# Keys turned by VectorE and by transfers instead of by TensorE, a third score bank, and weight units dealt out anew

## The reference, cut to what matters

```python
kx, vx = split(ctx_2048 @ w_kv_x.T)          # 4096 context rows, 8 groups of 128
kx = layernorm(kx, kxln_w, kxln_b)            # over the 128 of a head
p  = softmax(q @ kx.T / sqrt(128))            # 2 heads of a group share keys and values
out = p @ vx
```

## Time and profile before

| | us |
|---|---|
| median of 3 runs | 2565.9 (2561.31 to 2568.36) |
| the profiled execution | 2565.89, its span 2564.1 |
| TensorE busy | 2278.4 (89%) |
| VectorE busy | 1792.0 (70%) |
| ScalarE busy | 1193.7 (47%) |
| GpSimd busy | 589.8 (23%) |
| wide stage, first projection to last weighing | 195.96 to about 1170 |

### The profile page before, as it was taken

The page is one execution under the profiler, slowest core; times in us unless marked ns, Lnnn a source line. Parts: engine busy times, 40 slices in busy tenths (PEclk is TensorE's granted clock), DMA queues, the critical chain, the costliest instruction groups (busy, mean ns, idle before and its releaser), DMA issues. The chain is left out here.

```text
span 2564.1 us, 31522 instructions
## 1 busy us (share of the span) xinstructions
PE 2278.4 (89%) x11472; PEld 1555.9 (61%) x11472; DVE 1792.0 (70%) x3422; ACT 1193.7 (47%) x1924; POOL 589.8 (23%) x435
## 2 busy tenths in 40 slices
PE   3778999999999999886797989788878779899998
PEld 2556666666666666564685456555546337677876
DVE  7857977887687778977775976766767764554444
ACT  4443466556565666533233114576666853211111
POOL 7810033333333333441000003313141300000000
PEclk9889999999999999998898999999999989899999
DMA  3331100010100100003445100000000023555661
GB/s 132 115 139 54 54 17 29 14 32 9 29 17 22 29 9 25 5 1 131 156 158 218 68 21 10 1 10 1 6 5 1 21 79 139 216 202 220 232 236 66
DMA packets 48438, 187.98 MB, mean 73 GB/s; under 512 B 6112, under 2 KB 10976, under 8 KB 38048
## 3 DMA queue, kind: packets, MB, share of 16 engines
q1 hardware_dynamic: 48288, 186.00, 20.1%
HBM read 175.50 MB, written 10.49 MB: 73 GB/s over the span
## 5 line engine op out<-in xcount | busy, mean ns | idle before, releaser
L407 PE MATMUL wide_a<-wide_w,ctxT 128*128 128x256 f32 (+1 forms) x2048 | 436.9, 367 | 2.8 <-POOL wide_eps L376 2.8
L407 PEld LDWEIGHTS wide_a<-wide_w,ctxT 128*128 128x128 f32 x2048 | 367.9, 191 | 77.3 <-issue 36.5
L389 POOL TENSOR_TENSOR wide_sums<-wide_sums,wide_s 128x512 f32<-128x512 f32 x224 | 303.7, 1356 | 467.6 <-ACT wide_s L537 454.5
L432 PE MATMUL wide_scores<-wide_q,wide_keysT 128*128 128x512 f32 x512 | 242.2, 611 | 21.2 <-ACT wide_s L533 21.2
L442 PE MATMUL wide_o<-wide_s,wide_values 128*128 128x512 f32 x512 | 230.8, 594 | 3.5 <-ACT wide_s L537 3.5
L533 ACT COPY wide_s<-wide_scores 128x512 f32<-128x512 f32 x256 | 148.0, 585 | 174.8 <-PE wide_scores L432 166.5
L1814 DVE TENSOR_REDUCE int_peaks<-int_a 128x1 f32<-128x1024 f32 x128 | 156.2, 1223 | 92.9 <-PE int_a L1537 91.7
L1537 PE MATMUL int_a<-int_keys,int_qrows 96*128 96x512 bf16 x512 | 151.1, 392 | 58.4 <-DVE int_peaks L1814 32.3
L432 PEld LDWEIGHTS wide_scores<-wide_q,wide_keysT 128*128 128x128 f32 x512 | 88.8, 191 | 158.2 <-ACT wide_s L533 96.4
L1689 ACT ACTIVATE int_prob<-int_a,int_shift,int_qscale 128x1024 uint8<-128x1024 f32 x128 | 155.4, 1216 | 49.6 <-PE int_a L1537 49.3
L595 DVE TENSOR_TENSOR wide_top<-wide_top,wide_s 128x512 f32<-128x512 f32 x240 | 165.7, 691 | 17.1 <-ACT wide_s L533 11.4
...
## 6 DMA issues: line engine op xcount, KB each, us to landing
...
wide_unit<-hbm_ffn_units SPq DMA_DIRECT2D x30, 256.0 KB, 2.6
ffn_early<-wide_unit SPq DMA_DIRECT2D x30, 256.0 KB, 2.0
```

The source lines that it names most:

```text
L389: ins = pool.tensor_tensor(sums[0][:, :], before, part[:, j, :], ALU.add)
L407: mm = pe.matmul(a[h][:, j, cols], ctxT[:, kc, t * P:(t + 1) * P], w[g % 2][:, kc, cols], start=(kc == 0), stop=(kc == KC - 1))
L432: pe.matmul(sp_[j % 2][:, :], keysT[:, j, :], q[:, :], start=True, stop=True).then_inc(s_s, 1)
```

## The change

- TensorE's `turn` is gone. After normalising, VectorE transposes the keys of a step in squares of 32 x 32 into `squares`; SyncE stores these to DRAM (`send_squares`, 256 KB) and fetches them back in four transfers of 64 KB, one for each quarter of the partitions, with the squares' places exchanged (`fetch_keys`, pieces of 512 bytes). ScalarE's `keep_turned` becomes `scale_keys`, which reads the landed squares from SBUF, writes `keysT` and stands behind `keep(n, 1)`, not between the two.
- The bank of the turned keys becomes a third bank for scores, used in turn.
- Queries have two buffers; the loads of queries and weights move to later steps of a group.
- Units: `slots` has two halves in steps 1 to 7, one in steps 8 to 17 and then, as before, one in all steps but 2 and 3 of a group; the double slots in steps 0, 8 and 23 and a slot in step 60 go. 28 units instead of 30 are treated in the wide stage, 20 instead of 18 in the causal one, with `due` = 0, 2, 5, 7, 10, 12, 15, 17, 20 instead of 0, 3, 6, 8, 10, 12, 14, 16, 18.

```diff
@@ -46,7 +46,7 @@
 TOPG = 3
 EG = 8
 F_TILES = [(0, 128), (128, 128), (256, 96)]
-FFN_LATE = [7, 23] + [u + n for n in range(8, 16) for u in (0, 16)]
+FFN_LATE = [6, 22, 7, 23] + [u + n for n in range(8, 16) for u in (0, 16)]
 FFN_EARLY_UNITS = [n for first in (0, 16, 4, 20, 32, 36, 40, 44) for n in range(first, first + 4) if n not in FFN_LATE]
 FFN_EARLY = len(FFN_EARLY_UNITS)
 BATCH = 4
@@ -302,14 +302,16 @@
     VR, SR = LAG + 1, LAG - 1
     LATE = N - QPG
     COLS = 2 * TOK
-    halves_at = [1 if n <= 2 * QPG + 1 or n % QPG not in (2, 3) else 0 for n in range(N)]
-    for n in list(range(QPG + 1)) + [3 * QPG - 1]:
-        halves_at[n] = 2
-    slots = [n for n in range(N) for _ in range(halves_at[n])][:2 * FFN_EARLY]
+    slots = [n for n in range(1, QPG) for _ in range(2)] + list(range(QPG, 2 * QPG + 2))
+    slots += [n for n in range(2 * QPG + 4, N) if n % QPG not in (2, 3) and n != N - 4]
+    slots = slots[:2 * FFN_EARLY]
     with Stage(nc, "wide") as st:
-        q = st.sb("q", [P, COLS])
+        q = [st.sb(f"q{i}", [P, COLS]) for i in range(2)]
         keys = [st.sb(f"keys{i}", [P, 4, D]) for i in range(2)]
-        keysT = st.sb("keysT", [P, 4, P])
+        squares = st.sb("squares", [P, 4, 4, 32])
+        landed = st.sb("landed", [P, 4, 4, 32])
+        keysT = st.sb("keysT", [P, 4, 4, 32])
+        keys_dram = nc.dram_tensor("keys_by_squares", (2, P, 4, P), F32, kind="Internal").ap()
         values = [st.sb(f"values{i}", [P, 4, D]) for i in range(VR)]
         s = [st.sb(f"s{i}", [P, 4, COLS]) for i in range(SR)]
         top = st.sb("top", [P, COLS])
@@ -327,16 +329,17 @@
         unit = [st.sb(f"unit{i}", [P, DM]) for i in range(2)]
         unit_stat = st.sb("unit_stat", [P, 3, DM // 32])
         a = [st.ps(f"a{i}", [P, 2, 2 * D]) for i in range(2)]
-        sp_ = [st.ps(f"scores{i}", [P, COLS]) for i in range(2)]
-        b = st.ps("turned", [P, 4, P])
+        sp_ = [st.ps(f"scores{i}", [P, COLS]) for i in range(3)]
         o = [st.ps(f"o{i}", [P, COLS]) for i in range(2)]
         f = st.ps("rows", [P, 4, P])
-        s_ql = st.sem("q_loaded")
+        s_ql = [st.sem(f"q_loaded{i}") for i in range(2)]
+        s_sq, s_sent = st.sem("squares_turned"), st.sem("squares_stored")
+        s_back = [st.sem(f"keysT_loaded{i}") for i in range(2)]
         s_unit = [st.sem(f"unit_loaded{i}") for i in range(2)]
         s_early, s_stored = st.sem("unit_turned"), st.sem("unit_stored")
-        names = ("constants products kept var std normed turned keysT scores s_kept top topT peak rows peak_rows shifted exp summed "
+        names = ("constants products kept var std keysT scores s_kept top topT peak rows peak_rows shifted exp summed "
                  "weighed total half put values values_kept dve pool")
-        (s_c, s_a, s_kv, s_var, s_std, s_kn, s_t, s_kt, s_s, s_se, s_top, s_tt, s_pk, s_row, s_pr, s_sub, s_exp, s_sum,
+        (s_c, s_a, s_kv, s_var, s_std, s_kt, s_s, s_se, s_top, s_tt, s_pk, s_row, s_pr, s_sub, s_exp, s_sum,
          s_o, s_tot, s_half, s_put, s_vp, s_vk, s_dve, s_pool) = (st.sem(n) for n in names.split())
 
         with nc.Block() as block:
@@ -352,18 +355,40 @@
                     sp.wait_ge(s_early, i + 1)
                     sp.dma_start(early[i], unit[i % 2][:, :]).then_inc(s_stored, 16)
 
+                def load_queries(g):
+                    if g >= 2:
+                        sp.wait_ge(s_s, 4 * QPG * (g - 1))
+                    sp.dma_start(q[g % 2][:, :], q_dram[:, 2 * g:2 * g + 2, :].rearrange("p h n -> p (h n)")).then_inc(s_ql[g % 2], 16)
+
+                def send_squares(n):
+                    sp.wait_ge(s_sq, n + 1)
+                    if n >= 2:
+                        sp.wait_ge(s_back[n % 2], 64 * (n // 2))
+                    sp.dma_start(keys_dram[n % 2], squares[:, :, :, :].rearrange("p b t i -> p b (t i)")).then_inc(s_sent, 16)
+
+                def fetch_keys(n):
+                    sp.wait_ge(s_sent, 16 * (n + 1))
+                    if n >= 1:
+                        sp.wait_ge(s_kt, n)
+                    for c in range(4):
+                        sp.dma_start(landed[32 * c:32 * (c + 1), :, :, :].rearrange("p a t i -> p a (t i)"),
+                                     keys_dram[n % 2][:, c, :].rearrange("(a j) x -> j a x", j=32)).then_inc(s_back[n % 2], 16)
+
+                load_queries(0)
+                load_queries(1)
                 load_unit(0)
                 load_unit(1)
-                for n in range(N):
-                    if n % QPG == 0:
-                        g = n // QPG
+                for n in range(N + 1):
+                    if n >= 1:
+                        send_squares(n - 1)
+                        fetch_keys(n - 1)
+                    g = n // QPG
+                    if n % QPG == 1 and g + 1 < NG:
                         if g >= 1:
-                            sp.wait_ge(s_s, 4 * QPG * g)
-                        sp.dma_start(q[:, :], q_dram[:, 2 * g:2 * g + 2, :].rearrange("p h n -> p (h n)")).then_inc(s_ql, 16)
-                        if g + 1 < NG:
-                            if g >= 1:
-                                sp.wait_ge(s_a, 2 * QPG * g)
-                            sp.dma_start(w[(g + 1) % 2][:, :, :], wkv_dram[g + 1]).then_inc(s_w[(g + 1) % 2], 16)
+                            sp.wait_ge(s_a, 2 * QPG * g)
+                        sp.dma_start(w[(g + 1) % 2][:, :, :], wkv_dram[g + 1]).then_inc(s_w[(g + 1) % 2], 16)
+                    if n % QPG == 2 and 1 <= g and g + 1 < NG:
+                        load_queries(g + 1)
                     for i in [i for i in range(FFN_EARLY) if slots[2 * i + 1] == n - 1]:
                         store_unit(i)
                         if i + 2 < FFN_EARLY:
@@ -423,13 +448,13 @@
                 def score(n):
                     g, c = divmod(n, QPG)
                     if c == 0:
-                        pe.wait_ge(s_ql, 16 * (g + 1))
+                        pe.wait_ge(s_ql[g % 2], 16 * (g // 2 + 1))
                     pe.wait_ge(s_kt, n + 1)
                     for j in range(4):
                         i = 4 * n + j
-                        if i >= 2:
-                            pe.wait_ge(s_se, i - 1)
-                        pe.matmul(sp_[j % 2][:, :], keysT[:, j, :], q[:, :], start=True, stop=True).then_inc(s_s, 1)
+                        if i >= 3:
+                            pe.wait_ge(s_se, i - 2)
+                        pe.matmul(sp_[i % 3][:, :], keysT[:, j, :, :].rearrange("p a i -> p (a i)"), q[g % 2][:, :], start=True, stop=True).then_inc(s_s, 1)
 
                 def weigh(m):
                     g, c = divmod(m, QPG)
@@ -443,14 +468,6 @@
                                        start=(c == 0 and j == 0), stop=(c == QPG - 1 and j == 3))
                     mm.then_inc(s_o, 1)
 
-                def turn(n):
-                    pe.wait_ge(s_kn, n + 1)
-                    if n >= 1:
-                        pe.wait_ge(s_kt, n)
-                    for j in range(4):
-                        mm = pe.transpose(b[:, j, :], keys[n % 2][:, j, :], C["ident"][:, :])
-                    mm.then_inc(s_t, 1)
-
                 def turn_top(g):
                     pe.wait_ge(s_top, QPG * (g + 1))
                     if g >= 2:
@@ -483,8 +500,6 @@
                     g = n // QPG - 1
                     if n < N:
                         project(n, 0)
-                    if 1 <= n <= N:
-                        turn(n - 1)
                     if n % QPG == 1 and 0 <= g < NG:
                         turn_top(g)
                     if n % QPG == 2 and g >= 1:
@@ -507,7 +522,7 @@
                     act.wait_ge(s_a, 2 * n + h + 1)
                     if h == 0:
                         if n >= 2:
-                            act.wait_ge(s_t, n - 1)
+                            act.wait_ge(s_sq, n - 1)
                         if n >= VR:
                             act.wait_ge(s_o, n - VR + 1)
                     ins = act.copy(keys[n % 2][:, 2 * h:2 * h + 2, :], a[h][:, :, :D])
@@ -530,17 +545,18 @@
                     if j == 0 and n >= SR:
                         act.wait_ge(s_o, n - SR + 1)
                         act.wait_ge(s_sum, n - SR + 1)
-                    act.copy(s[n % SR][:, j, :], sp_[j % 2][:, :]).then_inc(s_se, 1)
+                    act.copy(s[n % SR][:, j, :], sp_[(4 * n + j) % 3][:, :]).then_inc(s_se, 1)
 
                 def exponential(m):
                     act.wait_ge(s_sub, m + 1)
                     act.activation(s[m % SR][:, :, :], s[m % SR][:, :, :], ACT.Exp, scale=scale).then_inc(s_exp, 1)
 
-                def keep_turned(n):
-                    act.wait_ge(s_t, n + 1)
+                def scale_keys(n):
+                    act.wait_ge(s_back[n % 2], 64 * (n // 2 + 1))
                     if n >= 1:
                         act.wait_ge(s_s, 4 * n)
```

(15 more changed lines are left out.)

## The result

The changed kernel takes 2600.4 us (median of 4 runs, 2595.8 to 2604.35) against 2565.9: a ratio of 1.0145, 95% interval 1.0129 to 1.0162. The prediction was 2593 (2547 to 2615), slower, with a chance of 0.70. The profiled execution has a span of 2598.5 us.

A forecast was written before the change was run, and what follows sets the result against it. TensorE was taken to bound the wide stage's middle, VectorE having a quarter to spare. Terms of -24 - 2.6 + 43 + 8.5 + 1.6 + 0.8 = +27 on 2565.9 gave 2593 us, range 2547 to 2615.

The forecast's parts named there:

- TensorE, -24: Wide stage, steps 10 to 55: without transposes (0.43) and the bank wait (0.09), 46 steps save 0.52 us each.
- Stalls of steps 21 and 24, -2.6: Wide stage: the double slot at step 23 goes; losses of 1.4 and 1.2 us behind steps 20 and 23 disappear.
- Chain of late steps, +43: Wide stage, steps 10 to 55: late VectorE work meets GpSimd's additions, stalling TensorE 6.9 to 9.7 us a group.
- Last group and drain, +8.5: Steps 56 on: VectorE sets the pace; eight added transposes, stretched instructions and late entry cost 6.1 to 12 us.
- Head, +1.6: Before step 10: VectorE's 11.68 us chain gains 0.76 in six steps, less halves that left steps 0 and 8.
- Causal stage, +0.8: Causal stage: two more units make VectorE late in some pairs of heads; an earlier first mask gives back 3.3 us.
- Transfers, nothing: Keys' trip through DRAM: about 6.3 us (5.0 to 14) hidden by 9.2 us of cover, costing nothing.
- A: Rival, chance 0.23: VectorE's extra work is hidden, extras slip past GpSimd's additions or stretches do not add; 2546 us.
- D: Rival, chance 0.07: gains and stalls cancel, 20 us less of stalls, within 0.3% (7.7 us) of 2566.
- B: Rival: keys return beyond 9.2 us of cover; a 10 us trip gives 2637 us; chance 0.06 together with C.
- C: Rival: the strided transpose takes twice its row, 0.7 us more on VectorE, 2635 us; chance 0.06 together with B.
- Signs: Expected in the new profile: groups of 120 to 122 us, VectorE near 90% busy, waits at steps 5, 6, 0, 1.

The follow-up runs named there:

- e6: Kernel before without TensorE's transposes of the keys (scaled unturned, nothing added on VectorE): 2542.0 us, ratio 0.9907.
- e3: Changed kernel without the weight units' halves on VectorE in the wide stage (units loaded and stored as they are): 2538.7 us, ratio 0.9894 to the kernel before.
- e3b: Kernel before without the weight units' halves on VectorE in the wide stage: 2549.7 us, ratio 0.9941.
- e5: Kernel before with only the change's new dealing of weight units (slots, late units, due list): 2561.0 us, ratio 0.9987.
- e1: Changed kernel with each of GpSimd's wide-stage additions covering 8 columns of 512: 2533.8 us, ratio 0.9873 to the kernel before.
- e2: Changed kernel without VectorE's transposes of the keys (constants go out and back, all waits stay): 2570.7 us, ratio 1.0014 to the kernel before.
- e7: Changed kernel with two score banks instead of three: 2590.1 us, ratio 1.0103 to the kernel before.
- f2: Changed kernel with the normalising of the keys moved to ScalarE, VectorE transposing after its subtraction: 2545.5 us, ratio 0.9929 to the kernel before.

## Why the prediction was right, by its own steps

The sum said +27, the runs +34.5. The direction and the main term were right; most of the difference is the head.

- **TensorE, -24.** Right: 0.44 a step for the transposes (e6) and 0.515 with the bank (e3 less e3b).
- **Stalls of steps 21 and 24, -2.6.** Right, 3.1 (e5). 
- **Chain of late steps, +43.** From step 10 to 50 the kernel lost 18.7 us (10.39 less 6.66, and 1.7, 6.5, 3.7 and 3.1). With 40 x 0.52 and 2.6 given up by the other two terms, the chain costs 42; the prediction had 39 for this part. The mechanism is shown: without GpSimd's additions (e1) or without the halves (e3) it is gone. Its inner sizes were less good, and that 39 came so near to 42 is in part luck. The waits that are there have the sizes worked out, but step 5 hardly waits (0.1) and step 0 only in two groups of four, so that a group's waits come to 5.1 or 7.0, against 6.9 to 9.7. What fills the gap is the lower clock behind some of them, 0.1 to 3.5 us a group, which the sum did not have (a group lost 7.2 to 10.6 against 112.47). e2 and e7 show the chain's rule to be coarse: it overrates what an earlier start gives back, and says the wrong sign for a bank.
- **Last group and drain, +8.5.** From step 50 on 7.8 (275.95 less 268.14), where the terms that touch this stretch had 9.2 (the 8.5, and 3.8 of chain less 3.1 of saving).
- **Head, +1.6.** This term failed in its mechanism: 6.7 by step 10. I took the 11.68 of the earlier trace rows for VectorE's chain alone and let VectorE's added 0.76 set the head. VectorE's chain is as long as that, but the kernel before keeps 11.67 without any halves (e3b). In the changed kernel TensorE's own path sets the 12.05: the scaling placed behind the second keep stands between a projection and the scores, with no weighing to cover it. The first trip of the keys, which nothing covers, and the lower clock behind it cost most of 4.5 more (1.7 of them lie in the first multiplies of this execution), and no term had them. The halves that left steps 0 and 8 gave back 3.7 (e5 reaches step 10 at 113.05, the kernel before at 116.73) where the sum had 3.0, so the move costs 10.3 in the head where it had 4.6; with VectorE relieved it is 9.7 (e3 less e3b).
- **Causal stage, +0.8.** Not to be told from what other kernels show there.
- **Transfers, nothing.** Right where the 9.2 us of cover are: no wait in the middle. Wrong at step 1, as said under the head. Whether the 4.4 us of ScalarE's waits in the last group cost TensorE anything is not shown.
- **Rivals.** A (2546) failed: the extras do not slip past GpSimd. D failed with it. B (keys late) and C (a transpose of over 1 us; it takes 0.71) are refuted by the trace. That a transpose isn't stretched could not be read from the earlier trace rows, where it starts 0.59 behind GpSimd's end; f2 shows it.
- **Signs.** A group of eight took 119.7 to 123.1, and VectorE was busy 96.85 of 112, 86% where I had said near 90. The wait at step 5 is missing, the one at step 0 in half of the groups.
